# Router of an AdaLN-FFN-MoE kernel: 64 products with 128-row weights in place of 256 row-tile products

## What is computed

```
y = conv_general_dilated(x, w, padding=[(K - 1, 0)], feature_group_count=C)   # K = 16 taps: z
logits = jnp.einsum('bsd,de->bse', z, Wr)                                     # the router, E = 8
w, sel = jax.lax.top_k(logits, 2)
gate = one_hot(sel) weighted by softmax(w)
out = sum over e of gate[..., e] * (z @ We[e] + be[e])
x = x + out
```

## Time and profile before

| | us |
|---|---|
| median of three runs | 831.52 |
| lowest and highest | 828.22, 833.4 |
| the profiled execution | 832.25 |
| its span, first to last instruction | 830.5 |

### The profile page before, as it was taken

The page is one execution under the profiler, slowest core; times in us unless marked ns, Lnnn a source line. Parts: engine busy times, 40 slices in busy tenths (PEclk is TensorE's granted clock), DMA queues, the critical chain, the costliest instruction groups (busy, mean ns, idle before and its releaser), DMA issues.

```text
span 830.5 us, 12599 instructions
## 1 busy us (share of the span) xinstructions
PE 737.6 (89%) x3954; PEld 431.8 (52%) x3954; DVE 564.7 (68%) x834; ACT 397.6 (48%) x635; POOL 476.9 (57%) x738
## 2 busy tenths in 40 slices
PE   1754599999999999999989999928899999999995
PEld 0112244444444444444436664326688888888884
DVE  2469999999998999998645441279753564545452
ACT  2056466667777777777612343215422434343432
POOL 1037889888888888886210000001457788888773
PEclk9987899999999999999999999958899999999998
DMA  9985147799999996554399899999459899999986
GB/s 359 387 318 164 26 89 141 142 182 178 180 173 167 183 192 129 131 115 90 83 215 225 94 114 239 130 79 322 114 102 166 146 167 165 167 165 168 164 162 89
DMA packets 230270, 137.50 MB, mean 166 GB/s; under 512 B 162798, under 2 KB 195054, under 8 KB 229054
## 3 DMA queue, kind: packets, MB, share of 16 engines
q1 hardware_dynamic: 210094, 99.94, 59.8%
q0 software_dynamic: 15456, 36.47, 24.2%
q10 hardware_dynamic: 4656, 0.30, 0.6%
HBM read 80.27 MB, written 35.42 MB: 139 GB/s over the span
## 4 chain that ended last, share of the span: by engine, by line
PE 58%; DVE 9%; DMA 7%; SPq 7%; POOL 7%; issue 7%; ACT 3%; POOLq 0%; DVEq 0%; ACTq 0%
PE PS L1597 21%; PE PS L1499 8%; PE PS L1448 6%; PE PS L1471 6%; PE PS L1460 6%; PE PS L1526 4%; PE PS L1577 3%; SPq L391 3%; DMA TZ<-in_taps 2%; DVE Ih L1094 2%; ACT Qh L827 1%; PE PS L1548 1%; DMA QyT<-Qy 1%; DMA QT<-Qh 1%; SPq L468 1%
## 5 line engine op out<-in xcount | busy, mean ns | idle before, releaser
L1597 PE MATMUL PS<-W,ZH 128*128 x552 | 178.4, 404 | 2.7 <-DVE ACC L1344 1.9
L751 POOL DMA_INDIRECT ZR<-z_scratch,IDG x69 | 69.2, 1003 | 154.9 <-DVE IDS L1315 134.2
L1448 PE MATMUL PS<-W,QyT 128*128 128x512 bf16 x512 | 123.8, 386 | 28.6 <-DMA QyT<-Qy 16.5
L760 POOL DMA_INDIRECT out_x<-YS,IDS x69 | 110.5, 1601 | 46.0 <-ACT YS L948 27.5
L1460 PE MATMUL PS<-W,QyT 128*128 128x512 bf16 x512 | 120.9, 379 | 0.0
L1471 PE MATMUL PS<-W,QT 128*128 128x512 bf16 x512 | 117.4, 383 | 3.5 <-DMA QT<-Qh 2.6
L948 ACT ACTIVATE YS<-YS,SG 128x512 f32<-128x512 f32 x69 | 50.1, 726 | 146.7 <-DVE YS L1376 146.7
L1597 PEld LDWEIGHTS PS<-W,ZH 128*128 128x128 f32 x552 | 99.5, 190 | 21.6 <-issue 3.9
L1597 PE MATMUL PS<-W,ZL 128*128 x276 | 109.0, 395 | 0.0
L1358 DVE TENSOR_TENSOR ZL<-PS,ZH 128x512 fp32r<-128x512 f32 x69 | 47.7, 691 | 78.4 <-ACT ZH L937 78.4
L1448 PEld LDWEIGHTS PS<-W,QyT 128*128 128x128 bf16 x512 | 49.4, 99 | 93.7 <-DMA QyT<-Qy 20.7
(11 more groups left out here) (230 smaller groups left out, 1062.7 us busy)
## 6 DMA issues: line engine op xcount, KB each, us to landing
XW<-out_x SPq DMA_DIRECT2D x64, 240.0 KB, 4.7
X<-in_x SPq DMA_DIRECT2D x32, 256.0 KB, 10.1
out_x<-X SPq DMA_DIRECT2D x32, 256.0 KB, 3.5
z_scratch<-ZZ SPq DMA_DIRECT2D x8, 1024.0 KB, 25.6
WRAW<-in_We SPq DMA_DIRECT2D x8, 1024.0 KB, 12.8
XR<-in_x SPq DMA_DIRECT2D x20, 256.0 KB, 4.3
stage<-in_w1T SPq DMA_DIRECT2D x4, 1024.0 KB, 7.9
stage<-in_w2T SPq DMA_DIRECT2D x4, 1024.0 KB, 12.3
```

What stands on the lines that cost most here:

```text
L751: pool.indirect_dma_start(ZR[m % UZ][:], None, z_d, bass.IndirectOffsetOnAxis(IDG[:, m:m + 1].bitcast(U32), 0)) \
L760: pool.indirect_dma_start(x1_d, bass.IndirectOffsetOnAxis(IDS[:, m:m + 1].bitcast(U32), 0), YS[m % UN][:], None, compute_op=ALU.add).then_ ...
L1448: i = nc.tensor.matmul(GP[:, a, :], QyT[t][:, k, :], W12[:, k, o:o + CH], start=(k == 0), stop=(k == KD - 1))
L1597: x = nc.tensor.matmul(bank[i], zz[i % 2][:, k, :], W2[:, bass.ds(q, 1), part, k, :].rearrange("p o d -> p (o d)"), start=(k == 0 and n == ...
```

## The change

ZZ's 128 partitions are now contracted by one product for each k, with 128x128 weights, and all 64 accumulate in one bank. The weights of a product hold 16 tokens times 8 experts as columns. WB therefore has 16 values s in place of 8, in two tiles of 32 feature pairs each, and takes 32 ScalarE instructions of 256 columns in place of 8 of 512. PM has 16 columns; SEL and its semaphore are gone. One bank is copied to LGS in place of four, and two products with the identity turn it. The wait on `z_done` ahead of the first product asks for 25 in place of 28, since only bank 0 has to be free.

```
--- before.py
+++ after.py
@@ -115,8 +115,8 @@
         ZW2 = HB2 * NP
         ZZ = place("ZZ", a_h - 4 * ZW2, [P, 5, HB2, NP])
         ZH2 = [ZZ[:, 4], ZZ[:, 0]]
-        WB = place("WB", 0, [P, NP, OH, E])
-        assert a_h - 4 * ZW2 == NP * OH * E
+        WB = [place(f"WB{i}", 12288 * i, [P, NP // 2, OB, E]) for i in range(2)]
+        assert a_h - 4 * ZW2 == NP // 2 * OB * E and 12288 == a_h - 3 * ZW2
         a_s = a_h + 4 * FF
         assert a + 2 * FF <= a_s
         Y = [place(f"Y{i}", a_s + D * i, [P, D]) for i in range(3)]
@@ -200,9 +200,8 @@
 
         a = a_s
         WRX = place("WRX", a, [P, NP, E])
-        PM = place("PM", a + D, [P, OH])
-        SEL = place("SEL", a + D + OB, [P, OH * E])
-        LGS = [place(f"LGS{g}", a + 2 * D + NCB * g, [P, NCB]) for g in range(NQ)]
+        PM = place("PM", a + D, [P, OB])
+        LGS = place("LGS", a + 2 * D, [P, NCB])
         BOH = [place(f"BOH{i}", a + CC * MT * i, [P, CC, 2, MT], BF16) for i in range(2)]
         a += CC * MT * 2
         ZDH, ZDL = (place(n, a + D * i, [P, KD, P], F32R) for i, n in enumerate(("ZDH", "ZDL")))
@@ -321,7 +320,7 @@
         oh_done, boh_done, num_done, tab_done, slots_done = sem("oh_done"), sem("boh_done"), sem("num_done"), sem("tab_done"), sem("slots_done")
 
         we_in = [sem(f"we_in{e}") for e in range(E // 2)]
-        wh_done, w_low, be_in, sel_done = sem("wh_done"), sem("w_low"), sem("be_in"), sem("sel_done")
+        wh_done, w_low, be_in = sem("wh_done"), sem("w_low"), sem("be_in")
         rows_free = sem("rows_free")
         zr_in = [sem(f"zr_in{i}") for i in range(UZ)]
         y_out = [sem(f"y_out{i}") for i in range(UN)]
@@ -894,8 +893,10 @@
                 if q == 0:
                     act.wait_ge(route_in, 32)
                     act.wait_ge(pm_done, 1)
-                if 0 <= q < OH:
-                    nc.scalar.activation(WB[:, :, q, :], WRX[:], ACT.Copy, scale=PM[:, q:q + 1]).then_inc(wb_done, 1)
+                for s in range(2 * q, 2 * q + 2) if 0 <= q < OB // 2 else ():
+                    for i in range(2):
+                        nc.scalar.activation(WB[i][:, :, s, :], WRX[:, NP // 2 * i:NP // 2 * i + NP // 2, :], ACT.Copy,
+                                             scale=PM[:, s:s + 1]).then_inc(wb_done, 1)
 
             def high(e):
 
@@ -1187,8 +1188,7 @@
             spread(3)
             for j in range(NQ):
                 halo(1, j)
-            nc.vector.tensor_reduce(PM[:], IDF[:].rearrange("p (g q j) -> p q g j", q=OH, j=NQ), AX.XY, ALU.add).then_inc(pm_done, 1)
-            nc.vector.tensor_tensor(SEL[:], IDF[:, 0:P // 2], IDF[:, P // 2:P], ALU.add).then_inc(sel_done, 1)
+            nc.vector.tensor_reduce(PM[:], IDF[:].rearrange("p (u s j) -> p s u j", s=OB, j=NQ), AX.XY, ALU.add).then_inc(pm_done, 1)
             for g in range(4, 2 * NG):
                 spread(g)
 
@@ -1228,8 +1228,7 @@
             for e in range(E // 2):
                 low(e)
             dve.wait_ge(lg_done, 1)
-            for g in range(NQ):
-                nc.vector.tensor_copy(LGS[g][:], bank[g][:, 0:NCB]).then_inc(lt_done, 1)
+            nc.vector.tensor_copy(LGS[:], bank[0][:, 0:NCB]).then_inc(lt_done, 1)
 
             def wide(m):
                 return m[:].rearrange("p (n o) -> p n o", o=1).broadcast_to([P, NT, E])
@@ -1516,23 +1515,16 @@
             for g in range(NG):
                 conv(1, g)
 
-            pe.wait_ge(wb_done, OH)
+            pe.wait_ge(wb_done, 2 * OB)
             for k in range(NP):
                 if k % 4 == 0:
-                    pe.wait_ge(z_done, max(NP // 2 - 4, NP // 4 + k // 4 + 1))
-                c = k % 2
-                for g in range(NQ):
-                    q = slice(QD * g, QD * g + QD)
-                    i = nc.tensor.matmul(PS[P // 2 * c:P // 2 * c + P // 2, g, 0:NCB], WB[q, k].rearrange("p q e -> p (q e)"),
-                                         ZZ[q, ::-4, :, k], start=(k < 2), stop=(k >= NP - 2))
+                    pe.wait_ge(z_done, max(NP // 2 - 7, NP // 4 + k // 4 + 1))
+                i = nc.tensor.matmul(bank[0][:, 0:NCB], WB[2 * k // NP][:, k % (NP // 2)].rearrange("p s e -> p (s e)"),
+                                     ZZ[:, ::-4, :, k], start=(k == 0), stop=(k == NP - 1))
             i.then_inc(lg_done, 1)
-            pe.wait_ge(lt_done, NQ)
-            pe.wait_ge(sel_done, 1)
-            for n in range(2 * 2):
-                o = HB2 * (n // 2)
-                for h in range(2):
-                    i = nc.tensor.matmul(bank[4][:, OH * E * n:OH * E * n + OH * E], LGS[2 * h + n % 2][:, o:o + HB2], SEL[:],
-                                         start=(h == 0), stop=(h == 1))
+            pe.wait_ge(lt_done, 1)
+            for h in range(2):
+                i = nc.tensor.matmul(bank[4][:, P * h:P * h + P], LGS[:, HB2 * h:HB2 * h + HB2], IDF[:], start=True, stop=True)
             i.then_inc(lb_done, 1)
 
 
```

## The result

| | before | after |
|---|---|---|
| median, us | 830.94 (4 runs, 828.22 to 833.4) | 847.39 (4 runs, 846.59 to 848.77) |
| the profiled execution | 832.25 | 847.36 |
| its span | 830.5 | 845.6 |
| its granted clock, mean | 0.962 | 0.964 |

The ratio is 1.0208, with a 95% interval of 1.0188 to 1.0228: 16.5 us slower, where no change was forecast. The time lies outside the range, between rivals 3 and 4.

A forecast was written before the change was run, and what follows sets the result against it. TensorE's chain from convolution through router was taken to bound the kernel until SyncE's loads. Loop 0.2, copies 1.0 and turn 2.4 us save 3.6, of which 0.5 survives: 831.7 us, 831.0 against the median, range 827.5 to 837.5 us.

The forecast's parts named there:

- rivals 3 and 4: Router loop slower: 348 ns a record, 835.9 us, chance 0.11; or 2.24 ns a column, 864.7 us, chance 0.13.
- What bounds the kernel: Convolution through router: TensorE holds nearly all the chain without waits, so a shorter router is a shorter chain, until loads meet it.
- this queue does not hang on the router: SyncE's queue of experts', BEB and ACC loads: the router's last product was long done when it issued at 560 us.
- The price of the loop: Router loop, line 1526: 1.12 ns per spread column, 286 ns a record, 36.6 us in all, 0.2 us shorter.
- rival 1: Router loop: spread columns cost a lone stream nothing, loop 27.4 to 30.8 us, but loads decide; 832.4 us, chance 0.16.
- The upper bound: Router loop: if side-by-side tiles read independently, a lone stream pays 2.24 ns a column, 573 ns a record, loop 73.4 us.
- The middle price: Router loop: 0.84 ns plus 0.52 ns spread cost, 1.36 ns a column, 348 ns a record, 44.6 us.
- The threshold of 379 ns: Router loop: the price per record from which the kernel would be slower by over 1% (8.3 us).
- The sum: Loop, copies and turn together: 0.2 + 1.0 + 2.4 = 3.6 us earlier at line 1238.
- The tail: Behind the loop: copies from 1.43 to 0.42 us, turn from 3.30 us to 0.9 us for four records.
- Building WB: ScalarE beside the convolution: 1.96 us per bank fits within 2.31 us; the build is hidden either way.
- Where 3.6 us go: Router to first slot: BEB and ACC loads and earlier gathers keep nearly all of the 3.6 us; gain taken as 0.5 us.

The follow-up runs named there:

- b2_one_tile: Kernel before, but the first 32 k go to the lower column tile, the last 32 to the upper, so one tile streams per quadrant: 846.9 us, ratio 1.0197.
- a2_steps: Changed kernel with router columns 1, 2, 4 and 32 words apart, each for a quarter of the 64 k: 834.57 us, a single execution.
- a1_adjacent: Changed kernel, each router product reading 256 adjacent words in place of words 64 apart: 829.69 us, ratio 0.9993.
- a5_short_tail: Changed kernel with adjacent columns for 43 of 64 k, so its loop is as long as the old one: 832.55 us, ratio 0.9978.
- d3_tail: Kernel before with a shorter sum: ScalarE copies two banks, VectorE adds the others, four products turn in place of eight: 832.59 us, ratio 1.0005.
- d1: Kernel before with d3_tail's shorter sum, gates' store on GpSimd, BEB ahead of experts 6 and 7, ACC on ScalarE's queue: 829.96 us, ratio 0.9971.
- d2: d1 plus GpSimd copying the last 16 k of z into an adjacent tile during the loop: 828.18 us, ratio 0.9925 to the kernel before.
- e1: Changed kernel with the gates' store moved from ScalarE to SyncE, behind BEB's load: 845.11 us, ratio 1.0114 to the kernel before.
- c1: b1_adjacent with queues rearranged: SyncE issues gates' store, experts 4 and 5, BEB, experts 6 and 7; ScalarE issues ACC: 828.95 us, ratio 0.9927.
- b1_adjacent: Kernel before, each row-tile router product reading 256 adjacent words in place of spread ones: 829.46 us, ratio 0.9986.

## Why the prediction was wrong

- **What bounds the kernel**: right. TensorE runs from the convolution through the router without a gap, and the loads wait behind. What was not weighed is that the two sides are unequal: a shorter router is given back, a longer one is paid. Nor does "this queue does not hang on the router" hold for a long one: in the changed kernel SyncE stood 19.0 us for line 1522 and issued the loads at its end.
- **The price of the loop**: this is the step that failed. It took 1.12 ns for a spread column as "paid by each record in turn", so 286 ns a record; it is 434 ns. Both rows behind the 1.12, the old router and the convolution, had two column tiles side by side. Their agreement across weight shapes and N did rule out the weight load. It could not tell a price paid in turn from one that two streams share, since neither row had one stream alone. The prediction named this very weakness in rival 1 ("both run two tiles at once"), but used it only for a faster loop. b2_one_tile shows that it cuts the other way: 1.64 ns a column for one tile at a time, and a loop of 53.63 us, with the old weights.
- **The upper bound** of 2.24 ns was right to be doubted: 434 ns is 0.76 of 573. The middle price, 348 ns, added the spread cost of a pair (2.24 - 1.72 = 0.52 ns) to a lone stream; in a2_steps and a1_adjacent that cost is 1.69 - 0.85 = 0.84 ns. Rivals 3 and 4 had the right sign and 0.24 between them, and the truth lay between them. The threshold of 379 ns for slower by over 1% was passed.
- **The sum** with 434 ns in it is 832.25 + 18.8 - 3.4 = 847.7 us, against 847.36 of the profiled execution. That this is so close is partly luck: +3.3 us between the logits and the first gather, nearly all from the gates' issue, and -1.3 us from there to z_low were in no term, and the convolution ended 1.75 us sooner.
- **Two slips in the working**: z_low at "about 585 to 587" against 585.22 is a loss of 0.9 us in its middle, so the gain of 0.5 us does not come out of it. Rival 1's z_low at 586.6 is 1.4 us late, so by the median of before it gives 832.9 us; 832.4 counts from the forecast. Neither moves the verdict.
- **The tail**: right. Copy and turn take 1.25 in place of 4.83 us, 3.6 us less, the copy 0.44 and the four records 0.73 (0.9 forecast).
- **Building WB**: right that it is hidden. The timeline of ScalarE has one bank's copy, four instructions of 256 columns and the next copy, 2.30 us apart:

```profile
471.06 0.59 ACT L890 COPY ZZ<-PS 128x512 f32<-128x512 f32 x1
471.54 1.73 ACT L898 ACTIVATE WB<-WRX,PM 128x256 f32<-128x256 f32 x4
473.36 0.58 ACT L890 COPY ZZ<-PS 128x512 f32<-128x512 f32 x1
```

  That is 0.48 + 1.73 = 2.21 us of a bank's 2.31; 1.96 was forecast. It fits with 0.1 us to spare.
- **Where 3.6 us go**: the claim that they bring next to nothing is right in a5_short_tail and d3_tail, its mechanism half right. The load of ACC does hold VectorE, 2.77 us in a5 and 7.99 us in a1. The other part was missed: the prediction has the store of the gates move 3.6 us ahead and lets it delay z's store, but as if its own issue stayed as long. In a5 it moves into z's store, and ScalarE pays for it (7.80 in place of 4.58 us) with the BOH copies queued behind. In the changed kernel itself the logits came 13 us late, SyncE had issued its loads at 556.59 us, ahead of the gates' store, which they lengthened to 7.47 us, and no load held z_low.
- **The two rules of the Trainium skill**: the line of 16 bytes ("Advanced Engine Details and Errata", Memory Cachelines) speaks against a gain in the loop, as was said, and a2_steps shows its step. From the speedup of up to 2 that "TensorEngine Tiling (Array Packing)", Theoretical Speedup, gives two small tiles came the estimate of 73.6 us for the new loop, where 55.6 were measured. For two adjacent tiles its factor of two holds (0.85 against 0.44 ns); for spread columns it is 1.5. It was the better guide to the sign.

What stays open: why two spread streams deliver 1.5 times one and not once or twice, whether it matters that products of one tile follow each other into the same bank, and what three or four spread tiles would do; no run tried that.

## What to carry to other kernels

A price that is read from two tiles running side by side is the price of the pair; before costing a lone stream with it, find a row with one stream, and if there is none, let the range reach to the whole price of a tile. When the reading of spread columns limits TensorE, as here, filling the array with bigger weights saved nothing and lost the overlap of the small ones (36.8 to 55.6 us); look at the distance between moving columns first, and at what can make them adjacent under cover. And where two chains meet, count a gain only up to the other chain, but a loss nearly in full.

## What the hardware showed beside that

- A float32 stream alone takes 0.85 ns for an adjacent column, 0.89 two words apart, 1.76 four words apart and 1.69 from 32 words on. Two side by side take 0.44 (adjacent) and 1.12 ns (64 words) between them. Weights read at such a distance cost a lone stream's 1.72 ns for each of their columns.
- Issuing the same two DMAs of the gates took 2.60 us on GpSimd (d1, d2), 3.79 to 9.54 us on ScalarE and 10.92 and 13.03 us on SyncE (e1, c1), and ScalarE's next copies waited meanwhile. Traffic alone does not set the length: ScalarE took 3.79 us at 300 GB/s (b2) and 7.80 us at 61 GB/s (a5).
- A loop of short records (b1_adjacent, 512 in 17.6 us of running) stood 9.3 us in three stops for nothing but issue, and the clock was granted at 0.71 and 0.50 behind two of them. The loop of 128 longer records with the same bytes to read (a1_adjacent) did not stand.
